# A mixture-of-experts block: down weights kept by expert, rows loaded through ACT's queue, all expert weights carried by each row

## The reference

```python
x = x + attention(layernorm(x))        # 4 sequences of 512 tokens, width 512, 16 heads of 32
# attention: q, k with rotary embedding and a layer norm per head,
# a = tril((q k^T) ** 4); out = (a / a.sum(-1)) v; out @ w_out
h = layernorm(x)                       # 2048 tokens
scores = sigmoid(h @ gate_weight.T); biased = scores + expert_bias        # 16 experts
# groups of 4: keep the 2 groups with the largest top-2 sum, then the 4 best experts
w = scores[chosen]; w = 2.5 * w / w.sum()
out = 0
for e in range(16):                    # we[e] is w where e was chosen, else 0
    out += we[e][:, None] * (silu(h @ gate[e].T) * (h @ up[e].T) @ down[e].T)   # inner width 256
x = x + out + silu(h @ sg.T) * (h @ su.T) @ sd.T                          # shared expert
```

## Time and profile before

| | us |
|---|---|
| median of 3 runs | 1303.08 (1302.91 to 1303.76) |
| the profiled execution | 1311.01 |
| its span | 1309.2 |

### The profile page before, as it was taken

The page is one execution under the profiler, slowest core; times in us unless marked ns, Lnnn a source line. Parts: engine busy times, 40 slices in busy tenths (PEclk is TensorE's granted clock), DMA queues, the critical chain, the costliest instruction groups (busy, mean ns, idle before and its releaser), DMA issues.

```text
span 1309.2 us, 20849 instructions
## 1 busy us (share of the span) xinstructions
PE 1003.3 (77%) x5650; PEld 478.3 (37%) x5651; DVE 766.3 (59%) x1574; ACT 516.5 (39%) x950; POOL 386.3 (30%) x525
## 2 busy tenths in 40 slices
PE   5957797655997646986548767688899999988873
PEld 2412245121444212451214433244444444444441
DVE  2867587864685845877745673344555555554542
ACT  2366334644236533346532423233334333333331
POOL 0036200456002554004561035113333333323322
PEclk9967898776996668976768788899999999999997
DMA  8015570254410354602444579958888988888874
GB/s 304 1 59 184 175 227 1 97 178 165 146 60 15 130 196 178 252 0 96 149 178 163 218 278 332 291 144 201 198 207 197 210 205 202 192 185 187 197 164 95
DMA packets 88353, 217.80 MB, mean 166 GB/s; under 512 B 9456, under 2 KB 10480, under 8 KB 86896
## 3 DMA queue, kind: packets, MB, share of 16 engines
q1 hardware_dynamic: 70384, 175.21, 39.8%
q0 software_dynamic: 17920, 42.04, 17.3%
HBM read 131.39 MB, written 85.82 MB: 166 GB/s over the span
## 4 chain that ended last, share of the span: by engine, by line
PE 27%; DMA 23%; issue 21%; POOL 11%; DVE 9%; ACT 5%; DVEq 1%; POOLq 1%; SPq 1%; ACTq 0%
DMA out<-yy,sidx 18%; PE bank L472 10%; POOL s_p L857 6%; PE bank L565 4%; PE bank L553 3%; POOL xs_scratch L843 3%; PE bank L602 2%; DMA xg<-xn_scratch 2%; PE bank L489 2%; PE bank L623 1%; DMA wd<-w_scratch 1%; PE bank L539 1%; DMA w_scratch<-arena 1%; PE bank L462 1%; ACT arena L751 1%
## 5 line engine op out<-in xcount | busy, mean ns | idle before, releaser
L602 PE MATMUL bank<-arena,xgT 128*128 (+1 forms) x1152 | 288.9, 388 | 8.2 <-ACT xgT L801 3.1
L857 POOL TENSOR_TENSOR s_p<-s_p,c_causal 128x128 f32<-128x128 f32 x256 | 160.8, 654 | 420.0 <-DVE s_p L1132 415.9
L553 PE MATMUL bank<-s_p,vtok 128*32 128x128 f32 (+3 forms) x512 | 124.7, 616 | 137.8 <-POOL s_p L857 99.2
L794 ACT ACTIVATE hT<-bank 128x512 f16<-128x512 f16 x96 | 57.3, 597 | 331.4 <-PE bank L612 331.4
L623 PE MATMUL bank<-wd,hT 128*128 128x512 f16 x576 | 147.3, 394 | 45.4 <-DMA wd<-w_scratch 24.7
L472 PE MATMUL bank<-arena 128*128 128x512 f32 x384 | 169.5, 600 | 2.3 <-issue 2.3
L751 ACT ACTIVATE arena<-bank 128x512 f32<-128x512 f32 (+3 forms) x256 | 97.9, 436 | 156.0 <-PE bank L539 129.5
L602 PEld LDWEIGHTS bank<-arena,xgT 128*128 128x128 f16 x1152 | 109.9, 100 | 135.4 <-issue 39.8
L1265 DVE TENSOR_TENSOR hh<-sg,bank 128x256 f32<-128x256 f32 x96 | 40.4, 421 | 177.2 <-ACT sg L810 176.9
L1132 DVE TENSOR_TENSOR s_p<-arena 128x512 f32<-128x512 f32 (+3 forms) x128 | 67.5, 547 | 118.5 <-ACT arena L751 114.8
L880 POOL DMA_INDIRECT out<-yy,sidx x80 | 125.2, 1565 | 19.8 <-issue 19.8
(11 more groups left out here) (150 smaller groups left out, 1284.0 us busy)
## 6 DMA issues: line engine op xcount, KB each, us to landing
wd<-w_scratch SPq DMA_DIRECT2D x82, 512.0 KB, 5.3
arena<-w_experts SPq DMA_DIRECT2D x34, 768.0 KB, 5.9
w_scratch<-arena SPq DMA_DIRECT2D x34, 768.0 KB, 4.5
xg<-xs_scratch SPq DMA_DIRECT2D x80, 257.0 KB, 2.7
arena<-w_scratch SPq DMA_DIRECT2D x17, 1024.0 KB, 9.5
xin<-x SPq DMA_DIRECT2D x5, 1024.0 KB, 8.3
xs_scratch<-spare SPq DMA_DIRECT2D x16, 257.0 KB, 7.7
arena<-x SPq DMA_DIRECT2D x4, 1024.0 KB, 5.9
```

What stands on the lines that cost most here:

```text
L553: mm = pe.matmul(bank[6 + n][r, P * kb:N], w, s_p4[:, (i - 1) % 2, j, 0:N - P * kb], start=(kb == 0), stop=(kb == MB - 1), skip_group_chec ...
L602: mm = pe.matmul(bank[2 + k][:], xgT[:, k, xh * EC + c, :], w, start=(c == 0 and xh + wh == 0), stop=(c == EC - 1 and xh == 1))
L857: pool.tensor_tensor(d, d, C["causal"][:], ALU.mult).then_inc(p4_masked, 1)
```

## The change

- `xrow` carries all 16 weights of its token (columns E+1 to E+16, `XW` = 529 instead of 514). DVE writes them once from `ws`; `w4` goes. A routed tile's output takes the column of its expert, whose number DVE reads from `expert_id`.
- The row writes have no rounds and no `row_weights`: POOL waits for `places_ready` once, then issues the 16 scatters, in batches 1 to 3 two or three after the masks of each i from 9 to 15 (2, 2, 2, 3, 2, 2, 3), in the last batch one after the other.
- Down weights lie in a ring of four slots. SP loads them once for each expert; expert e waits until the last tile of expert e-4 has been through down (`done_at`) and until the load before has landed. PE reads the expert's number and slot (`wd_slot`) before each down.
- Routed rows of tiles TB+4 and on are loaded by ACT, between silu of t and the copy `xgT` of t+1; SP loads those of the first four.
- The last four pieces of the weight split move from t = 0 to 3 to t = 5 to 8 of the shared stage, on ACT and on DVE.

```diff
@@ -48,8 +48,9 @@
 TB = T // P
 RT = T * TOPK // P + NX
 NT = TB + RT
-XW = E + 2
+XW = E + 1 + NX
 CAPR = T + P
+RING = 4
 XROWS = NX * CAPR + NX * P
 XS, WS = 1024.0, 256.0
@@ -332,16 +335,14 @@
             def load_rows(t):
 
                 q = t.quarter
-                if not t.below(4) and t.below(TB + 4):
-                    sp.wait_ge(gT_ps, t.at(-3))
                 if t.shared():
+                    if not t.below(4):
+                        sp.wait_ge(gT_ps, t.at(-3))
                     sp.dma_start(xg[:, q, 0:E].bitcast(I32), xn_dram[t.at() * P:t.at() * P + P, :]).then_inc(rows_in[q], 16)
                     return
-                at = sp.value_load(row_off[0:1, bass.ds(t.at(-TB), 1)], min_val=0, max_val=XROWS - P)
-                if t.below(TB + 4):
-                    sp.wait_ge(h_ready, t.at(-3))
-                else:
-                    sp.wait_ge(numbers, t.at(-1 - TB))
+                at = sp.value_load(row_off[0:1, t.lo - TB:t.lo - TB + 1], min_val=0, max_val=XROWS - P)
+                sp.wait_ge(gT_ps, t.at(-3))
+                sp.wait_ge(h_ready, t.at(-3))
                 sp.dma_start(xg[:, q].bitcast(I32), xs_dram[bass.ds(at, P), :]).then_inc(rows_in[q], 16)
 
@@ -388,16 +389,18 @@
                 sp.wait_ge(y_sb, t.at(1))
                 sp.dma_start(out[bass.ds(t.at() * P, P), :], yy[:, t.par]).then_inc(fin_out[t.par], 16)
 
-            def load_down(t):
-
-
-                k = t.par
-                e = 0 if t.shared() else sp.value_load(expert_id[0:1, bass.ds(t.at(-TB), 1)], min_val=0, max_val=NX)
-                if not t.below(2):
-                    sp.wait_ge(y_ps, t.at(-1))
-                sp.dma_start(wd[:, k].rearrange("p h c n -> p h (c n)"),
-                             w16_dram[bass.ds(e * P, P), :, EC:NC6, :].rearrange("p h c n -> p h (c n)")
-                             ).then_inc(wd_in[k], 16)
+            def load_down(e):
+
+                if e > RING:
+                    done = sp.value_load(done_at[0:1, e - RING - 1:e - RING], min_val=TB, max_val=NT)
+                    sp.wait_ge(y_ps, done)
+                elif e == RING:
+                    sp.wait_ge(y_ps, TB)
+                if e:
+                    sp.wait_ge(wd_in, 16 * e)
+                sp.dma_start(wd[:, e % RING].rearrange("p h c n -> p h (c n)"),
+                             w16_dram[e * P:e * P + P, :, EC:NC6, :].rearrange("p h c n -> p h (c n)")
+                             ).then_inc(wd_in, 16)
 
             def shared_step(t):
@@ -431,24 +434,19 @@
                 elif t - 1 - APART == SPLIT:
                     load_expert(NX)
 
-            def routed_step(t):
-                if not t.is_(NT - 2) and not t.is_(NT - 1):
-                    load_rows(t.plus(2))
-                load_down(t)
-
             sp.wait_ge(ids_ready, 1)
             sp.wait_ge(spare_out, 16 * NX)
             sp.wait_ge(scattered, 16 * (B * MB * TOPK + NX))
             load_rows(Tile(None, TB))
             load_rows(Tile(None, TB + 1))
+            load_down(1)
             store_result(Tile(None, TB - 2))
-            routed_step(Tile(None, TB))
+            load_rows(Tile(None, TB + 2))
+            load_down(2)
             store_result(Tile(None, TB - 1))
-            for t in range(TB + 1, TB + 4):
-                routed_step(Tile(None, t))
-            tile_fours(sp, TB + 4, NT - 4, routed_step)
-            for t in range(NT - 4, NT):
-                routed_step(Tile(None, t))
+            load_rows(Tile(None, TB + 3))
+            for e in range(3, NX + 1):
+                load_down(e)
 
         @block.tensor
@@ -614,13 +612,17 @@
 
             def down(t):
                 k = t.par
+                if not t.shared():
+                    e = pe.value_load(expert_id[0:1, bass.ds(t.at(-TB), 1)], min_val=1, max_val=NX)
+                    slot = pe.value_load(wd_slot[0:1, bass.ds(t.at(-TB), 1)], min_val=0, max_val=RING - 1)
+                pe.wait_ge(wd_in, 16 if t.shared() else e * 16 + 16)
                 pe.wait_ge(hT_sb, t.at(1))
-                pe.wait_ge(wd_in[k], 16 if t.shared() else t.plus(-TB).uses(1) * 16)
                 if not t.below(2):
                     pe.wait_ge(y_sb, t.at(-1))
                 for c in range(FC):
                     for hh_, wh in ((0, 0), (0, 1), (1, 0)):
-                        mm = pe.matmul(bank[5 + k][:], hT[:, k, hh_ * FC + c, :], wd[:, k, wh, c, :],
+                        w = wd[:, 0, wh, c, :] if t.shared() else wd[:, bass.ds(slot, 1), wh, c, :]
+                        mm = pe.matmul(bank[5 + k][:], hT[:, k, hh_ * FC + c, :], w,
                                        start=(c == 0 and hh_ + wh == 0), stop=(c == FC - 1 and hh_ == 1))
                 mm.then_inc(y_ps, 1)
@@ -800,6 +802,13 @@
                     act.wait_ge(gu_ps, t.at(-1))
                 act.activation(xgT[:, k], oct16(bank[k]), ACT.Copy).then_inc(gT_sb, 1)
 
+            def load_rows(t):
+
+                q = t.quarter
+                at = act.value_load(row_off[0:1, bass.ds(t.at(-TB), 1)], min_val=0, max_val=XROWS - P)
+                act.wait_ge(numbers, t.at(-1 - TB))
+                act.dma_start(xg[:, q].bitcast(I32), xs_dram[bass.ds(at, P), :]).then_inc(rows_in[q], 16)
+
             def step(t):
                 k = t.par
                 if not t.is_(0):
@@ -808,13 +817,15 @@
                 if not t.below(2):
                     act.wait_ge(up_used, t.at(-1))
                 act.activation(sg[:, k], bank[2 + k][:, 0:FF], ACT.Silu, scale=1.0 / (XS * WS)).then_inc(silu_done, 1)
+                if not t.below(TB + 2) and not t.is_(NT - 2) and not t.is_(NT - 1):
+                    load_rows(t.plus(2))
                 if not t.is_(NT - 1):
                     copy_T(t.plus(1))
 
             act.wait_ge(xn16_ready, B)
             copy_T(Tile(None, 0))
 
-            all_tiles(act, step, lambda t: split_next(B, t) if t < 4 else None)
+            all_tiles(act, step, lambda t: split_next(B, t - 5) if 5 <= t < 9 else None)
             copy_hidden(Tile(None, NT - 1))
 
@@ -827,44 +838,31 @@
             pool.drain()
             pool.memset(spare[:], 0.0).then_inc(memset_done, 1)
             pool.wait_ge(consts_in, 16 * NCST)
-            ROUND = 16 * MB
-
-            def row_weights(b, k):
-
-                if k == 0:
-                    pool.wait_ge(places_ready, b + 1)
-                else:
-                    pool.wait_ge(scattered, b * (ROUND * TOPK) + k * ROUND)
-                pool.tensor_tensor(xrow[:, :, E + 1], w4[:, :, k], ones[:, 0:MB], ALU.mult).then_inc(tails, 1)
-
-            def place_rows(k):
-
-                for m in range(MB):
+            def place_rows(first, last):
+
+                for n in range(first, last):
+                    m = n % MB
                     pool.indirect_dma_start(out=xs_dram, out_offset=bass.IndirectOffsetOnAxis(
-                        ap=place_id[:, m, k:k + 1], axis=0), in_=xrow[:, m].bitcast(I32), in_offset=None).then_inc(scattered, 16)
+                        ap=place_id[:, m, n // MB:n // MB + 1], axis=0), in_=xrow[:, m].bitcast(I32), in_offset=None
+                        ).then_inc(scattered, 16)
 
             def sequence(b, before):
                 for i in range(NG * MB):
-                    k = i - 9
-                    if before is not None and 0 <= k < TOPK:
-                        row_weights(before, k)
                     for j in range(HG):
 
                         pool.wait_ge(p4_done[j % 2], b * (NG * MB * 2) + (2 * i + j // 2 + 1))
-                        if before is not None and 0 <= k < TOPK and j == HG - 1:
-                            pool.wait_ge(tails, before * TOPK + (k + 1))
+                        if before is not None and i == 9 and j == 0:
+                            pool.wait_ge(places_ready, before + 1)
                         d = s_p4[:, i % 2, j, 0:P]
                         pool.tensor_tensor(d, d, C["causal"][:], ALU.mult).then_inc(p4_masked, 1)
-                    if before is not None and 0 <= k < TOPK:
-                        place_rows(k)
+                    if before is not None and i >= 9:
+                        place_rows((i - 9) * 16 // 7, (i - 8) * 16 // 7)
 
             sequence(0, None)
             with pool.Fori(0, B - 1) as r:
                 sequence(r + 1, r)
-            for k in range(TOPK):
-                row_weights(B - 1, k)
-                pool.wait_ge(tails, (B - 1) * TOPK + (k + 1))
-                place_rows(k)
+            pool.wait_ge(places_ready, B)
+            place_rows(0, MB * TOPK)
             pool.wait_ge(ids_ready, 1)
             for e in range(NX):
@@ -1023,6 +1021,7 @@
                 dve.tensor_tensor(ws[:], ws[:], tmp4[:, 0:MB].unsqueeze(2).to_broadcast([P, MB, NX]), ALU.mult)
                 dve.drain()
 
+                dve.tensor_scalar(xrow[:, :, E + 1:XW], ws[:], ROUTE_SCALE, None, ALU.mult)
                 oh = oh4[:].rearrange("p (m k e) -> p m k e", m=MB, k=TOPK)
```

(14 more changed lines are left out.)

17 lines of the change are left out of this document (10 added, 7 removed).

## The result

The changed kernel takes 1289.34 us (median, 1287.58 to 1291.43), the kernel before beside it 1303.42 (1302.91 to 1304.12): ratio 0.9892, 95% interval 0.9872 to 0.9912. It is faster, by 14.1 us or 1.1%; forecast were 46.5, and the time lies above the range. The profiled execution of after took 1291.43 us, its span is 1289.7.

What follows compares the result with a forecast made beforehand. Bounds: row-write rounds in attention, transfers in the shared stage, serial adds and down-weight waits in routed tiles. From the 1303.1 us median, -42.9 - 2.6 - 7.0 + 6.0 = -46.5 gave 1256.6 us, range 1212 to 1280.

Steps and rivals of the forecast that it cites:

- the step from the profiled execution to the median: Whole kernel: the median of before lies 7.9 us under the profiled 1311.0, and all gains are subtracted from that median, 1303.1.
- 34.7 us a batch: Attention, batches 1 to 3: masks of i = 9 to 15 without rounds take this long, 42.9 us less in all.
- 3 x 0.9: Attention, DVE: weights by rank (1.18 us a batch) leave, a write of about 0.2 comes; 2.6 us less over three batches.
- the prediction's estimate of that price: Attention: if DVE's port held each of 39 issues for half its length, 25 us of gain would go; not in the sum.
- Rival B: Attention: POOL keeps the path, masks and issues alternate with nothing hidden, 46.8 us a batch; kernel 1292.9 us, chance 0.12.
- PE's two register reads before down: Routed tiles: they fall in gaps of the longer tile and cost nothing; about 0.3 us each without that cover.
- ACT's chain alone: Routed tiles: silu, register read, issue, copy, gate and up make 5.58 us a tile; 438.0 us in all, 6.0 more.
- The 7 us for gaps that close: Shared stage: row writes start earlier without gaps, so DMA engines fill sooner; 7 us less, bounds -13.2 to +4.
- The price of the store's wait for DVE's piece: Shared stage: SP's store now waits for DVE's split piece of t = 8, costing up to 4 us.
- A (ACT's read overlaps): Routed tiles: ACT's register read is hidden and only the issue shows, 5.08 us a tile; kernel 1218.6 us, chance 0.14.
- C (the adds): Routed tiles: serial adds landing in 7.4 us delay ACT's copy and PE, 58 us more; kernel 1314.8 us, chance 0.04.
- D: Routed tiles: down-weight loads were hidden, so dropping them gives nothing; no difference to the sum, counted in the forecast's 0.70.

Runs made afterwards that it cites:

- e18: The kernel before with one edit: POOL works out the row numbers ahead of its waits for the other parity's add and the output; 1271.7 us, ratio 0.9747.
- e6: The changed kernel with one register read on PE per routed tile instead of three, rows still issued ahead of the copy; 1274.1 us, ratio 0.9777.
- e14: e12 with two more register reads on PE ahead of down in each routed tile, values unused; 1222.8 us, ratio 0.9340.
- e17: The changed kernel with row numbers early and ACT issuing rows a tile ahead, behind the copy; three reads, row writes back to back; 1231.9 us, ratio 0.9410.
- e13: e10 with ACT issuing the rows of tile t+3 instead of t+2 behind its step of tile t; 1217.4 us, ratio 0.9307.
- e5: The changed kernel with ACT issuing rows behind the copy and PE doing one register read per routed tile instead of three; 1267.2 us, ratio 0.9719.
- e1: The changed kernel with the last batch's row writes in groups of four, each waiting for the landing of the one before; 1280.1 us, ratio 0.9789.
- e8: e5 with the last batch's row writes in groups of four, each behind the landing of the one before; 1257.1 us, ratio 0.9645.
- e9: e8 with the 16 writes of spare rows also in groups of four, each behind the landing of the one before; 1261.2 us, ratio 0.9652.
- e2: The changed kernel with ACT issuing the routed rows behind the copy of t+1 instead of between silu and that copy; 1283.7 us, ratio 0.9833.
- e4: The kernel before with only the rows part: 16 weights a row, no rounds; down weights loaded per tile, rows through SP; 1270.8 us, ratio 0.9748.
- e3: The changed kernel with both the last batch's row writes in groups of four and ACT's row load behind the copy; 1279.4 us, ratio 0.9805.
- e7: e4 with the last batch's row writes in groups of four, each behind the landing of the one before; 1262.6 us, ratio 0.9668.
- e10: e8 with POOL working out the row numbers of tile t+2 ahead of its waits for the add and the output; 1251.8 us, ratio 0.9595.
- e12: e7 with POOL's row numbers early, as in e10; down weights per tile, rows through SP; 1226.6 us, ratio 0.9401.
- e11: The changed kernel with 11 further 1 MB copies, DRAM to DRAM, on SP's queue in the shared stage, nothing waiting for them; 1291.8 us, ratio 0.9899.

## Why the prediction was wrong

The sum took off 32.7 us too much (1289.3 against 1256.6). In the terms of the traces: routed tiles 14.5, shared stage 10.8, the step from the profiled execution to the median 5.8, attention 1.5, the rest 0.2.

**Attention: right.** Forecast were 34.7 us a batch, measured 34.0 to 34.2; up to the first silu 44.0 us went where 45.5 were expected. (The working's 3 x 0.9 is 2.7 and not 2.6, and its 1.18 less 0.2 would give 2.9 for three batches; neither matters.) By the Trainium skill (SBUF — State Buffer, the note on the "DVE blocks DMA" trap) POOL can't write descriptors while DVE holds the port that they share; the prediction's estimate of that price was 25 us. The trace shows little of it: two of the nine issues between 614 and 636 us are over 1.4 us long where the others are 1.0, and all but 1.5 us of the gain came. Rival B fell with it.

**From the profile to the median: a step that was taken too lightly.** The profiled execution of before was 7.9 us over the median, and the forecast subtracted its gains from the median unchanged; the trace of after is only 2.1 over. e18 has the attention of before word for word. Its masks of i = 9 to 15 take 45.8, 46.2 and 48.5 us where the earlier trace rows have 49.1, 48.1 and 49.8, 6.5 us less, and its first silu comes 9.9 us earlier. So the length of the rounds differs between executions, and the profile showed a long one: likely, from one further trace, and not shown. The median was the weaker base: it came from three executions within 0.9 us, while 35 later ones spread over 17.9 us with medians 2 to 7 us higher. A part of this term is luck of the draw.

**Routed tiles: the chain was right, the cover was not.** The failing step is "PE's two register reads before down ... fall in gaps that the longer tile has: nothing." Taking them away (e6) gives an adds' stretch of 439.6 us, and the forecast for ACT's chain alone was 438.0; with them it is 452.5. So that step was off by 12.9 us, and the rest of the term by 1.6. Part of this closeness is luck: the copy starts 1.29 us behind silu in the median where 1.40 were forecast, a tile of 5.47 and not 5.58, and some 10 us of other delays, which the forecast had put at nothing, make up for it. The step named its own condition, the cover, and priced its absence at about 0.3 us a read, 47 us for two reads in 79 tiles; 13 to 20 were measured, so a part was covered. A read takes 0.30 us for the load, and more for what follows on the sequencer (the source view of the line in after):

```profile
L616 PEldq TENSOR_LOAD <-expert_id x80: 297/303/1000, 822.0 to 1270.1; - x80
```

In e14 two reads with unused values cost nothing. An explanation is the lead of PE's sequencer over its array: in the changed kernel the sequencer stands at gate and up until ACT's late copy is there, so it comes to the reads late, and down waits. But no run measures that lead, and it isn't the whole: in e17, where the copy is on time, the two extra reads, whose values the wait and the addresses need, still cost 15.9 us over e13's one. What of that is the address operations behind the reads isn't separated here. That the reads in these kernels cost 13 to 20 us is shown three times (e6, e5, e17); why e14's are free stays open.

**Shared stage: the gain of the gaps is there in one trace and lost in another.** The 7 us for gaps that close failed in after: +3.8. In e17, with the same row writes, the stage is 10.6 us shorter than before, inside the bounds given (-13.2 to +4). What differs is the hold between 713 and 757 us. It goes with PE's late completion signals: after and e1 to e8 have 7 to 12 of them in the stage, before and e9 to e18 none. Where they are and writes go back to back, the stage is 125.3 to 129.8 us long (after, e2, e4, e5, e6), with groups of four 117.5 to 122.2 (e1, e3, e7, e8); where they aren't, 115.4 back to back (e17) and 118.2 to 119.0 in groups (e10, e12, e13, e14). So by these traces, with e17 as the only one of its kind, the groups don't pay by themselves, they limit the hold. No edit decides between the two: e8 has the hold and e9 and e10 do not, and the three have the same instructions up to there. It is the early sets that have it and the later ones that don't, so it may belong to the executions and not to the kernels; the chip by itself doesn't explain it, since e5 to e8 have it and e17 doesn't, all on chip 4. What causes it stays open. The price of the store's wait for DVE's piece, up to 4 us, fits. SP's queue (start, from the first to the end of the last issue), against the earlier trace rows:

```profile
770.29 4.55 SPq L327 DMA_DIRECT2D w_scratch<-arena  x2
782.30 0.33 SPq L341 DMA_DIRECT2D xg<-xn_scratch  x1
```

The two stores are 3.2 us further apart than before (4.55 against 1.38), and the landing behind them takes 7.5 us instead of 14.6 (the prediction's 15.9 counts from the first store's start).

**What bounds the kernel now: a reading that was missed.** The prediction named serial adds and the wait for down weights for the routed stage of before, and took its 62 us over 4.63 a tile as things that ACT's longer chain covers. In sum that held, but the cause was another, and it was on the page: "L876 POOL ... 318.9 <-DMA out<-yy,sidx 154.2". That line was shown ahead of the prediction, and its working didn't use it. The numbers of tile t+2 were worked out behind the wait for an add's landing, though nothing in them needs it; SP's next load of rows waited for them 188.3 us in all, and the down weights stood in the same queue behind. Moving the numbers, with their wait for the rows, ahead of the other waits gives 35.9 us of the 427.5 (e18). In the changed kernel this was not tried by itself.

**The rivals.** A (ACT's read overlaps) fell: 1.29 us in the median stand between silu and copy. C (the adds) fell: POOL waits 24.9 us for landings from 850 to 1250 us, their median is 4.7. D's claim holds to within a few us: e12, which still loads the down weights for each tile, needs 4.5 us more in the routed stage than e13, which doesn't. e4, with rows on SP's queue and no ring, is 20 us better in the routed stage than the changed kernel, and where both are freed of the other chains ring and move together are worth those 4.5 us, or 9.2 by the medians. The Trainium skill (DMA: Bandwidth & Descriptors, Issuing engines are not separate DMA queues) had said that moving an issue to another engine saves no more than the sequencer's own time; these runs agree, though none has the ring with the rows on SP's queue.

## What to carry to other kernels

Before a stage is sped up, list every chain whose period is near the tile's: here the routed tile took 5.4 to 5.7 us in the mean with POOL's numbers, ACT's in-order queue or PE's reads in the way, so each edit to the changed kernel alone moved the routed stage by nothing (e2) or by 13 us (e6), and the traffic that the change removed set none of them. A signal that frees a buffer must stand ahead of every wait that it doesn't need; look for a cheap instruction with a long idle time before it. Don't put a register read on a busy engine at nothing: here two of them cost 13 to 20 us in three pairs and nothing in a fourth. A DMA issued from a compute engine is as late as that engine's place for it.

## What the runs showed of the hardware that was not expected

- PE's completion signals came late, by the trace's modelled ends: by 6.96 us behind the transposes of 717.61 and by 23.8 behind those that end at 735.43 (e1's expectation says up to 30 us, but nothing in that trace that waits for such a signal starts more than 23.8 us behind). They come in the traces of after and e1 to e8, all from the earlier sets, and not in those of before and e9 to e18, while the scatters are issued or shortly behind, and up to there e8, e9 and e10 have the same instructions.
- The DMA engines moved 318 GB/s in the row writes' window in after, 356 in e17 and 391 with e11's copies, and PE ran more in e11's window than in after's, not less. 11 MB more made the shared stage 1.8 us longer than after's and 16.2 us longer than e17's.
- The same rounds of row writes took 45.8 to 48.5 us a batch in one trace and 48.1 to 49.8 in another.
